# Squares of the queries as a bf16 part and a bf16 remainder, in the last two attentions of a four-layer network

## The reference

```
# third attention: B, S, SE = 1, 256, 512 in its own call; NH 16, NKV 4, HD 128
def _rmsnorm(x, w, eps=EPS):
    var = jnp.mean(xf * xf, axis=-1, keepdims=True)
    return (xf * jax.lax.rsqrt(var + eps)) * w
q = (hidden_states @ Wq + bq).reshape(b, s, NH, HD).transpose(0, 2, 1, 3)
k = (encoder_hidden_states @ Wk + bk) ...;  v = (encoder_hidden_states @ Wv + bv) ...
q = _rmsnorm(q, qn_w);  k = _rmsnorm(k, kn_w)
probs = softmax(q k^T * scale + mask);  out = (probs v) @ Wo
# fourth attention: the same with q = rms_norm(x @ Wq.T), then _rope(q, positions),
# and keys and values of the context and of x together
```

## Time and profile before

| | |
|---|---|
| time, three runs | 1301.7, 1304.97, 1305.1 us, median 1304.97 |
| span of the profiled execution | 1280.3 us |
| its own time | not listed apart from the three; the median is 24.7 us above the span |
| TensorE busy, matmul | 1137.0 us (89%) |
| TensorE weight loads | 846.0 us (66%) |
| VectorE, ScalarE, GpSimd busy | 848.7, 619.5, 352.7 us |
| squares matmuls | 256 rows in each attention, 35.7 and 34.7 us |

### The profile page before, as it was taken

One profiled execution on the slowest core, in us unless ns is written; L12 is line 12 of the kernel. 1 busy time (PEld: TensorE's weight loads), 2 busy tenths in 40 slices (PEclk: granted clock), 3 DMA queues, 4 the chain that ended last, 5 costly groups with the idle time before them and its releaser, 6 DMA issues.

```text
span 1280.3 us, 22884 instructions
## 1 busy us (share of the span) xinstructions
PE 1137.0 (89%) x8124; PEld 846.0 (66%) x8147; DVE 848.7 (66%) x1920; ACT 619.5 (48%) x1407; POOL 352.7 (28%) x328
## 2 busy tenths in 40 slices
PE   4866869899968999889999988999998999999894
PEld 3554644444445665889989755777667888888653
DVE  7788966787767684355556568544587777775664
ACT  5575534566734324344343343222466766666252
POOL 0040011222103002123122125777413333333032
PEclk9657977899968999989999979999998999999998
DMA  8010025000024224200000073633551000000100
GB/s 262 2 44 1 1 113 233 1 2 1 2 82 137 75 103 174 67 1 1 1 1 1 1 281 137 227 102 103 178 214 67 18 17 18 18 10 9 50 1 33
DMA packets 44571, 89.30 MB, mean 70 GB/s; under 512 B 7280, under 2 KB 30448, under 8 KB 42672
## 3 DMA queue, kind: packets, MB, share of 16 engines
q1 hardware_dynamic: 39184, 73.45, 15.9%
q0 software_dynamic: 5280, 14.42, 3.5%
HBM read 68.72 MB, written 21.10 MB: 70 GB/s over the span
## 4 chain that ended last, share of the span: by engine, by line
PE 65%; DVE 19%; ACT 5%; issue 5%; DMA 3%; POOL 2%; SPq 0%; DVEq 0%; ACTq 0%; POOLq 0%; PEldq 0%
PE psum L2146 4%; PE psum L3175 4%; PE psum L2558 4%; PE psum L2118 4%; PE psum L3147 4%; PE psum L2578 3%; PE psum L1694 2%; PE psum L1298 2%; PE psum L3095 2%; PE psum L2071 2%; PE psum L3117 2%; PE psum L3137 2%; PE psum L1273 2%; PE psum L3482 2%; PE psum L2049 2%
## 5 line engine op out<-in xcount | busy, mean ns | idle before, releaser
L1363 ACT ACTIVATE c_probs<-psum 128x512 f32<-128x512 f32 x128 | 75.1, 602 | 45.8 <-PE psum L1284 45.8
L1464 DVE TENSOR_REDUCE c_max<-psum 128x2 f32<-128x512 f32 x128 | 81.6, 678 | 22.0 <-PE psum L1273 21.0
L3175 PE MATMUL psum<-a_wo,a_outT 128*128 128x256 f32 x256 | 75.1, 405 | 0.7 <-DVE x_tok L3357 0.7
L2558 PE MATMUL psum<-m_experts,m_tileT 128*128 x188 | 63.7, 461 | 1.7 <-DVE m_tileT L2795 1.7
L2200 ACT ACTIVATE a_probs<-a_probs,a_max 128x64 f32<-128x64 f32 x128 | 42.7, 334 | 44.9 <-DVE a_max L2256 44.9
L3255 ACT ACTIVATE a_probs<-psum,a_max,a_q_rstd 128x128 f32<-128x128 f32 x128 | 56.8, 458 | 10.8 <-DVE a_max L3305 10.7
L2118 PE MATMUL psum<-ctxT_yT_hi,a_wq 128*128 128x128 f32 x256 | 52.8, 290 | 8.2 <-DVE a_qT L2242 7.1
L2242 DVE TENSOR_TENSOR a_qT<-psum,a_columns 128x512 f32<-128x512 f32 x32 | 22.0, 688 | 55.4 <-PE psum L2118 55.4
L2182 ACT ACTIVATE a_q_squares<-a_qT 128x512 f32<-128x512 f32 x32 | 20.1, 628 | 78.0 <-DVE a_qT L2242 77.6
L1694 PE MATMUL psum<-m_w,m_tileT 128*128 x120 | 54.5, 597 | 2.6 <-DVE m_tileT L1888 2.6
L3147 PE MATMUL psum<-ctxT_yT_hi,a_wq 128*128 128x128 f32 x256 | 52.4, 288 | 4.8 <-DVE a_q_cos L3316 4.1
(11 more groups left out here) (576 smaller groups left out, 3380.8 us busy)
## 6 DMA issues: line engine op xcount, KB each, us to landing
m_w<-m_w SPq DMA_DIRECT2D x8, 1536.0 KB, 14.5
m_experts<-m_e SPq DMA_DIRECT2D x16, 608.0 KB, 12.4
a_wq<-a_wq SPq DMA_DIRECT2D x2, 2048.0 KB, 10.5
m_rows_back<-m_back SPq DMA_DIRECT2D x4, 1024.0 KB, 8.9
a_ctx_kv<-a_ctx_k_v SPq DMA_DIRECT2D x8, 512.0 KB, 4.4
ctxT_yT_hi<-f_gate_up SPq DMA_DIRECT2D x2, 1024.0 KB, 7.5
a_v<-a_ctx_kv SPq DMA_DIRECT2D x16, 128.0 KB, 2.7
a_wo<-a_wo SPq DMA_DIRECT2D x1, 2048.0 KB, 7.8
```

The source lines that it names most:

```text
L1363: e.activation(c1P[:, n % 8, :, :], ps[:, 2 + n % 2, :].rearrange("p (k t) -> p k t", k=2), ACT.Exp, scale=float(1.0 / np.sqrt(np.float32( ...
L1464: e.tensor_reduce(c1M[:, u % 2, j, :], ps[:, c1_score_bank(n), :].rearrange("p (q t) -> p q t", q=2), AX.X, ALU.max).then_inc(c1_mx, 1)
L2558: ins = e.matmul(ps[:, 4 + t % 2, 0:M2_UP], m2xT[:, t % 2, kc, :], m2e[:, bass.ds(own + kc * M2_UP, M2_UP)], start=(kc == 0), stop=(kc == ...
L3175: ins = e.matmul(ps[:, 7, 0:D], a3at[:, i % 2, h, :, :], a3wo[:, h, :], start=(h == 0 and g is None), stop=(h == HQ - 1), skip_group_check ...
```

## The change

The f32 squares stay in `a2qs` and `a3qs`. Beside them ScalarE writes the squares rounded to bf16 (`qsh`): in the third attention by a second Square of the same queries, in the fourth by a copy of the f32 squares after the swapped halves. GpSimd subtracts that from the f32 squares and writes the remainder in bf16 (`qsl`), as the first item of its slot. Both lie in the memory of `y_tok`, which is free between the start of the attention and its end. TensorE sums both parts: eight bf16 matmuls in place of four f32 ones, all of them ahead of the slot's output products. It now waits for the remainder (`a2_ql`, `a3_ql`).

```diff
+        q_parts = yt[:, :, :].rearrange("p t d -> p (t d)").bitcast(BF16).rearrange("p (x g n) -> p x g n", x=2, g=QQ)
+        qsh, qsl = q_parts[:, 0, :, :], q_parts[:, 1, :, :]
...
@@ a2_pe, out_and_squares (a3_pe alike)
                 if g is not None:
-                    e.wait_ge(*a2_qf.at(g + 1))
+                    e.wait_ge(*a2_ql.at(g + 1))
+                    for k in range(4):
+                        b2, p_ = k // 2, 2 * (g % 4) + k % 2
+                        at_ = D + (p_ // 4) * 8 + (p_ % 4) * 2 + b2
+                        s_ = b2 * 256 + (k % 2) * P
+                        for x, part in enumerate((qsh, qsl)):
+                            ins = e.matmul(ps[:, 7, at_:at_ + 1], part[:, g % 4, s_:s_ + P], onesb[:, 0:1], start=(c == 0 and k == 0 and x == 0),
+                                           stop=(x == 1), skip_group_check=True)
+                    ins.then_inc(a2_sp.sem, 1)
                 if u is not None:
                     i = u // 4
                     e.wait_ge(*a2_o.at(2 * i + 1 + c // 2))
                     if c == 0 and i:
                         e.wait_ge(*a2_res.at(i))
-                for k in range(4):
-                    if g is not None:
...
-                        ins = e.matmul(ps[:, 7, at_:at_ + 1], a2qs[:, g % 4, s_:s_ + P], onesf[:, 0:1], start=(c == 0 and k == 0), stop=True,
-                                       skip_group_check=True)
...
-                    if u is not None:
+                    for k in range(4):
                         h = 4 * c + k
@@ a2_act, query_squares
-                e.activation(a2qs[:, g % 4, :], a2qT[:, g // 4 % 2, g % 4, :], ACT.Square).then_inc(a2_qf.sem, 1)
+                e.activation(a2qs[:, g % 4, :], a2qT[:, g // 4 % 2, g % 4, :], ACT.Square)
+                e.activation(qsh[:, g % 4, :], a2qT[:, g // 4 % 2, g % 4, :], ACT.Square).then_inc(a2_qf.sem, 1)
@@ a2_pool, at the head of each slot (a3_pool alike, waiting for a3_qh)
+                if a2_group(n, 1 - A2_AHEAD) is not None:
+                    g = n + A2_AHEAD - 1
+                    e.wait_ge(*a2_qf.at(g + 1))
+                    e.tensor_tensor(qsl[:, g % 4, :], a2qs[:, g % 4, :], qsh[:, g % 4, :], ALU.subtract).then_inc(a2_ql.sem, 1)
@@ a3_act, queries
-                e.activation(a3qs[:, g % 4, :], ps[:, bank, :], ACT.Square)
+                e.activation(a3qs[:, g % 4, :], ps[:, bank, :], ACT.Square).then_inc(a3_q32.sem, 1)
...
                 e.activation(a3f[64:128, g % 2, :], ps[0:64, bank, :], ACT.Copy).then_inc(a3_qf.sem, 1)
+                e.wait_ge(*a3_q32.at(g + 1))
+                e.activation(qsh[:, g % 4, :], a3qs[:, g % 4, :], ACT.Copy).then_inc(a3_qh.sem, 1)
```

31 lines of the change are left out of this document (15 added, 16 removed).

## The result

| | before | changed |
|---|---|---|
| median of 20 runs, same chip | 1304.51 us (1300.74 to 1313.99) | 1299.45 us (1292.13 to 1303.23) |
| ratio, 95% interval | | 0.9943 [0.9925, 0.9961] |
| profiled execution, its span | | 1301.65, 1299.9 us |

By the ratio the kernel became about 7 us faster (5 to 10; the medians lie 5.1 us apart), where 19.5 were forecast, with a range of 1277 to 1298. The prediction was wrong. One run of a later experiment ("one part") took 1804.05 us at a granted clock of 0.55 and is left out as a slow run.

The account below looks back on a forecast made before the run. TensorE was taken to bound the attentions' slots with output products, and a VectorE, ScalarE, GpSimd chain the others. -22.0 + 2.0 + 0.5 = -19.5 us, from 1304.97 to 1285.5 us, range 1277 to 1298.

Parts of the forecast that it names:

- Matmuls, 40 slots, -22.0: TensorE's slots with output products: eight bf16 squares matmuls replace four f32 ones, gaining 0.55 us a slot, 22.0 us.
- Conversions in the 40 slots at nothing: ScalarE's and GpSimd's added operations in slots with output products lie beside TensorE and cost nothing.
- The cover that I reckoned as 1.2 us: Third attention's slots: with the subtraction ahead of GpSimd's power and scaling, 1.2 us stay before VectorE reads the roots.
- the meeting: GpSimd's subtraction beside VectorE's two-input operations: 0.35 to 0.83 us each, 7 to 17 us in the fourth attention's slots, hidden.
- Starts, +2.0 and +0.5: The 24 slots without output products: third attention 2.0 us longer (-2 to +5), fourth 0.5 us longer (-3 to +4).
- part 3: Prediction's step on the 24 slots without output products: TensorE's saving mostly falls into waits for VectorE; +2.0 and +0.5 us.
- Half spacing: Rival: bf16 loads on TensorE take half the f32 spacing, 0.053 us; gain 14.0 us, time 1293.5; chance 0.11.
- no gain: Rival: eight squares loads take 96 ns each, plus 2.5 us of starts; time 1307.5; chance 0.05.
- the better start: Rival: both stretches without output products come out at their good ends (-5); time 1278; chance 0.08.
- a bound on VectorE or ScalarE: Rival: either engine becomes the bound in the fourth attention, half of its 11 us lost; time 1291; chance 0.12.
- TensorE waiting behind the power: Rival: squares wait for the remainder, late behind GpSimd's queries' power; slower, up to 1330 us; chance 0.04.
- The signs that I named: Expected: squares run 0.2 us, products 1.73, clock 1.00; wrong if run reaches 0.5, y_tok waits, or short stretches grow over 5.

Follow-up runs that it names:

- one part: Changed kernel with squares as one bf16 part: four bf16 matmuls a slot, no remainder, no added ScalarE operation; 1281.14 us against 1307.25 before, ratio 0.9774.
- Late groups: Changed kernel, but groups 0 to 11 of each attention keep f32 squares without conversion; 1262.67 us against 1285.53 before, ratio 0.9818.
- converted, not used: Changed kernel, all groups converted, but TensorE reads groups 0 to 11 in f32 without waiting for the parts; 1274.69 us against 1285.53 before, ratio 0.9925.

## Why the prediction was wrong

- **Matmuls, 40 slots, -22.0: right in kind, too small in size.** Measured are -10.4 and -10.6 us over 2 x 19 slot lengths, 21.0 together, against 20.9 forecast. That they agree so well is luck, for two errors cancel. Without the remainder the same slots return 12.5 and 11.5 us, 24.0 together: 6.05 to 5.39 us (0.66 a slot) in the third attention, 10.04 to 9.43 (0.61) in the fourth, where I had 0.55. The subtraction takes the other 3 us back. The run of eight takes 0.22 us as read from the earlier trace rows. The recorded length of a load is 99 and 96 ns in the two attentions, which shows again that it is not the spacing. The Trainium skill (TensorE: Matmul & The Clock Gate, section Weight-path perf modes) has the fast path at about 2x as measured; with the 107 ns of the same page's section LDWEIGHTS that is an estimate of 53 ns. One part and two show half of that.
- **Conversions in the 40 slots at nothing: 3 us short.** The cover that I reckoned as 1.2 us for the maxima is short: every fourth slot of the third attention took 6.24 to 6.59, against 5.89 without the subtraction, 2.1 us in 19 slots (109.65 against 107.54). In the fourth it was 0.9 (134.1 against 133.2). VectorE's cover held, 114.96 busy of 134.30 us. I had put the meeting at 7 to 17 us of VectorE's time there; between the squares of slots 7 and 26 its busy time went from 101.58 to 114.77, 13.2 us, and stayed hidden.
- **Starts, +2.0 and +0.5: the step that failed.** Measured +3.6 and +5.4, 9.0 in place of 2.5, the second beyond its end of +4. That is 6.5 of the 9.7 us by which the sum of -19.5 missed the -9.8 of the traces. For the third, part 3 had the power behind two subtractions hold the maxima, which it does (5.7 us in two waits), and let savings elsewhere pay for it. For the fourth I followed only the first two subtractions to the first keys and then assumed that the chain waits for VectorE anyway, so that the conversions cost next to nothing. Late groups and converted, not used show the opposite: the conversions of groups 0 to 11 carry the whole loss, with the same matmuls on TensorE. In the fourth attention they made the start 6.5 us longer (74.8 to 81.3), about 4 of it TensorE's waiting and 2.4 busy time at a lower granted clock (0.90 against 0.93). In the third it was 3.3 us, 1.0 and 2.4. The prediction had the clock only as the bad end of the third's start (+5) and not in its sum. TensorE's longer wait for VectorE (9.4 us for 4.1) is no measure of the loss: in one part it is 9.9 and the start is shorter than before, since shorter matmuls turn into waiting.
- **The ends, +1.5 and +0.7**, were left out of the sum (2.2 us), which also counted slot 26's gain (1.0). Without the remainder they are 36.1 and 40.5 us, against 35.2 and 40.6 before and 36.7 and 41.3 changed. So the subtraction has a part in them; the rest stays open.
- **Rivals.** Half spacing and no gain are refuted by the run with one part, the better start by the table. For a bound on VectorE or ScalarE at most the 0.9 us of the fourth attention's slots are left, not half of the gain. TensorE waiting behind the power did not happen in the changed kernel's long stretches; it did as soon as the subtraction was moved back.
- **The signs that I named.** A run of 0.2 us, 1.8 us of products and the clock at 1.00 came true. "If the short stretches grow by over 5 us" was the true alarm: they grew by 9.0. Waits for y_tok came too, but only in the starts: 2.1 us in the third attention, 4.2 in the fourth.

## What to carry to other kernels

Split the program by what bounds it and apply a conversion only where the engine that it relieves is the bound. Here the 20 groups in TensorE-bound slots gave all the gain, and the 12 others gave 9 of its 21 us back; left alone, they cost nothing (ratio 0.9818 against 0.9887 on the same chip). When an operation is added to an engine that works in order, list what stands behind it and who waits for that in the first rounds too, and look for a wait on both sides before moving it: ahead of the powers it held VectorE, behind them TensorE. Before a longer stretch is put down to waits, compare TensorE's busy time and granted clock over it too.

## What the runs showed of the hardware

- Eight bf16 loads of 128 x 128 beside one-column matmuls follow each other in 0.027 us (0.22 for eight, 0.11 for four), though each is recorded with 96 to 99 ns.
- A GpSimd subtraction with SBUF inputs beside a VectorE addition with two SBUF inputs costs both: 0.69 to 1.53 us on VectorE, 1.16 to 1.60 on GpSimd. The Trainium skill (SBUF — State Buffer, section Who interferes with whom) states that such a pair contends, and the traces agree; with the subtraction held back, the addition was 691 to 693 ns in all 32 cases.
- The same matmuls in the third attention's start took TensorE 54.49, 55.54 and 57.58 us of busy time at a granted clock of 0.92, 0.89 and 0.87.
- Between the attentions, where all kernels have the same code, it took 207.5 to 209.9 us on three of the chips of the experiments and 233.3 to 239.8 on the fourth. A span of one chip and a time of another can't be subtracted.
